# Gated experts in transposed form: a tile's input weights copied by ScalarE and held stationary

## The reference

```python
def _L2_ffn_ref(hidden_states, gate_w, gate_up_proj, down_proj):
    x = hidden_states.reshape(-1, H)
    probs = jax.nn.softmax(x @ gate_w.T, axis=-1)
    w, idx = jax.lax.top_k(probs, TOP_K)
    w = w / jnp.sum(w, axis=-1, keepdims=True)
    combine = jnp.zeros((T, E), x.dtype).at[jnp.arange(T)[:, None], idx].add(w)
    def step(acc, inputs):
        gup, dn, ce = inputs
        g, u = jnp.split(x @ gup.T, 2, axis=-1)
        acc = acc + ce[:, None] * (jax.nn.silu(g) * u @ dn.T)
        return (acc, None)
...
x = x + jnp.tanh(g_ffn[2]) * _L2_ffn_ref(_layernorm(x, axis=-1), L2_ffn_gate_w, L2_ffn_gate_up_proj, L2_ffn_down_proj)
```

## Time and profile before

| | |
|---|---|
| median of 3 runs | 841.63 us (841.47 to 844.58) |
| the profiled execution, whole | 842.73 us |
| its span, first to last instruction | 840.9 us |
| mean granted TensorE clock | 0.919 of full |
| layer-2 gated stage, first gather to last scatter's issue | 479.35 to 561.64 us |
| layer-3 gated stage, the same | 754.09 to 827.65 us |
| busy: TensorE, its weight loads, VectorE | 81%, 63%, 50% of the span |
| busy: ScalarE, GpSimd | 35%, 27% of the span |

### The profile page before, as it was taken

How to read it: one execution, slowest core, us unless ns; L and a number is a source line. 1 busy time by engine, 2 the same in 40 slices (tenths; PEclk the granted TensorE clock), 3 DMA queues, 4 the chain that set the end, 5 groups by cost and what they waited for, 6 DMA issues and landing times. The chain is left out here.

```text
span 840.9 us, 15319 instructions
## 1 busy us (share of the span) xinstructions
PE 677.8 (81%) x5100; PEld 532.3 (63%) x5101; DVE 419.4 (50%) x1095; ACT 291.2 (35%) x827; POOL 229.4 (27%) x275
## 2 busy tenths in 40 slices
PE   3988789677989999996898899961967999887772
PEld 2657677357879999985467756640544676674431
DVE  3585447684645344426695533325654454352233
ACT  1286123574024533530441033320631444312220
POOL 2033000132144444221001156523500111116652
PEclk9999999799899999998996999995996999889896
DMA  7980000000210001001930111110000000001123
GB/s 236 336 324 2 1 0 1 1 2 1 64 45 20 27 21 26 14 17 55 364 102 1 32 38 41 41 49 21 2 1 1 2 3 2 1 29 45 41 41 91
DMA packets 28998, 44.96 MB, mean 53 GB/s; under 512 B 5458, under 2 KB 18402, under 8 KB 28674
## 3 DMA queue, kind: packets, MB, share of 16 engines
q1 hardware_dynamic: 24514, 35.02, 12.4%
q0 software_dynamic: 4416, 9.05, 4.1%
HBM read 37.44 MB, written 6.62 MB: 52 GB/s over the span
## 5 line engine op out<-in xcount | busy, mean ns | idle before, releaser
L1120 PE MATMUL experts_ps<-experts_act,experts_own 128*128 128x128 f32 x736 | 86.0, 275 | 0.0
L1120 PEld LDWEIGHTS experts_ps<-experts_act,experts_own 128*128 128x128 f32 x736 | 84.0, 192 | 0.1
L1278 PE MATMUL gated_ps_in<-experts_w_in,gated_slots_t 128*128 x138 | 71.1, 624 | 14.0 <-DVE gated_slots_t L1365 5.9
L1167 ACT ACTIVATE experts_act<-experts_ps,experts_b 128x128 f32<-128x128 f32 x184 | 52.6, 369 | 73.0 <-PE experts_ps L1120 52.1
L1050 POOL DMA_INDIRECT gated_slots<-ffn_tokens,keep_ffn_token x46 | 44.5, 968 | 69.4 <-issue 44.8
L648 POOL TENSOR_TENSOR core_e<-core_e,core_inverse 128x1024 f32<-128x1024 f32 x16 | 30.4, 1902 | 105.8 <-DVE core_inverse L794 105.8
L1197 DVE COPY experts_own<-experts_w 128x2048 f32 x23 | 28.2, 1227 | 57.4 <-PE experts_ps L1120 57.4
L1365 DVE COPY gated_slots_t<-gated_ps_x 128x128 f32<-128x128 f32 x46 | 13.4, 291 | 85.4 <-PE gated_ps_x L1270 70.4
L1041 POOL DMA_INDIRECT ffn_results<-gated_results,keep_ffn_row x46 | 45.4, 986 | 36.8 <-DVE gated_results L1375 28.6
L1050 POOL DMA_INDIRECT experts_slots<-ffn_tokens,keep_ffn_token x23 | 36.1, 1570 | 65.7 <-PE experts_ps L1101 43.6
L1297 PEld LDWEIGHTS gated_ps_y<-experts_w_out,gated_gated_t 128*128 128x128 f32 x276 | 35.3, 195 | 24.7 <-issue 24.7
(11 more groups left out here) (398 smaller groups left out, 1432.7 us busy)
## 6 DMA issues: line engine op xcount, KB each, us to landing
experts_w<-in_L_ffn_W SPq DMA_DIRECT2D x1, 8192.0 KB, 40.8
experts_w_in<-in_gated_in SPq DMA_DIRECT2D x1, 4096.0 KB, 12.2
combine_mine<-ffn_results SPq DMA_DIRECT2D x12, 256.0 KB, 3.6
experts_w<-in_L_ffn_W SPq DMA_DIRECT2D x1, 2048.0 KB, 13.1
experts_w_out<-in_gated_out SPq DMA_DIRECT2D x1, 2048.0 KB, 16.7
ffn_tokens<-route_xn SPq DMA_DIRECT2D x3, 512.0 KB, 3.2
experts_w_in<-in_L_ffn_gate_w SPq DMA_DIRECT2D x1, 1024.0 KB, 19.5
experts_w_in<-in_L_ffn_up_w SPq DMA_DIRECT2D x1, 1024.0 KB, 23.0
```

What stands on the lines that cost most here:

```text
L1120: mm = pe.matmul(ps_2[u][:, c * P:(c + 1) * P], own2[:, u, k, c * P:(c + 1) * P], act1[:, u, k, :], start=(k == 0), stop=(k == chunks - 1))
L1167: act.activation(to[:, u, c, :], source[u][:, c * P:(c + 1) * P], ACT.Gelu, bias=bias[:, bass.ds(e * chunks + c, 1)]).then_inc(done, 1)
L1278: mm = pe.matmul(ps_in[:, banks * u + n], slots_t[:, u, :], w_in[:, bass.ds(e, 1), 512 * n:512 * n + 512].rearrange("d a h -> d (a h)"), s ...
```

## The change

Only `gated_experts` changes, with two helpers that go. The input matmuls change roles: for each 128 gate or up columns the weights are stationary and the turned slots stream, so the result comes out transposed already, gate and up columns on the partitions. `turn`, `gated_t`, `ps_t` and `keep_gated` go. The stationary weights come from `own`, a buffer of two tiles that ScalarE fills by copying the tile's 1024 (layer 3: 512) columns out of `w_in`, at first for tiles 0 and 1 and then, behind each silu(j), for tile j + 2, once the input matmuls of tile j are done. TensorE loads an expert index only in `down`, ScalarE one for each copy. The outputs have two PSUM banks. VectorE's order is now multiply(j), keep_result(j - 1), keep_slots(j + 2), and TensorE's up(j + 1), turn_slots(j + 2), down(j). All tiles are written out; there are no hardware loops.

```diff
@@ gated_experts @@
-        gated, gated_t = s.sb("gated", [P, 2, width]), s.sb("gated_t", [P, 2, chunks, P])
+        own, gated = s.sb("own", [P, 2, 2 * chunks, P]), s.sb("gated", [P, 2, chunks, P])
-        ps_in = s.psum("ps_in", [P, 2 * banks, 512])
-        ps_x, ps_t, ps_y = s.psum("ps_x", [P, 512]), s.psum("ps_t", [P, 512]), s.psum("ps_y", [P, 512])
+        ps_in = s.psum("ps_in", [P, 2, banks * 512])
+        ps_x, ps_y = s.psum("ps_x", [P, 512]), s.psum("ps_y", [P, 2, 512])
...
-                def up(j, u, first=False):
-                    e = expert_index(pe, routes, j)
+                def up(j):
+                    if j >= TILES:
+                        return
                     pe.wait_ge(sem["slots_kept"], j + 1)
-                    if not first:
+                    pe.wait_ge(sem["own_kept"], j + 1)
+                    if j >= 2:
                         pe.wait_ge(sem["gated_ready"], j - 1)
-                    for n in range(banks):
-                        mm = pe.matmul(ps_in[:, banks * u + n], slots_t[:, u, :],
-                                       w_in[:, bass.ds(e, 1), 512 * n:512 * n + 512].rearrange("d a h -> d (a h)"),
+                    for c in range(2 * chunks):
+                        mm = pe.matmul(ps_in[:, j % 2, c * P:(c + 1) * P], own[:, j % 2, c, :], slots_t[:, j % 2, :],
                                        start=True, stop=True)
                     mm.then_inc(sem["in_made"], 1)
 
-                def turn(j, u, first=False):
+                def down(j):
+                    e = expert_index(pe, routes, j)
                     pe.wait_ge(sem["gated_ready"], j + 1)
-                    if not first:
-                        pe.wait_ge(sem["gated_kept"], j)
+                    if j >= 2:
+                        pe.wait_ge(sem["result_kept"], j - 1)
                     for c in range(chunks):
-                        mm = pe.transpose(ps_t[:, c * P:(c + 1) * P], gated[:, u, c * P:(c + 1) * P], keep.identity[:])
-                    mm.then_inc(sem["gated_turned"], 1)
...
+                        mm = pe.matmul(ps_y[:, j % 2, 0:D], gated[:, j % 2, c, :],
                                        w_out[:, bass.ds(e, 1), c, :].rearrange("d a h -> d (a h)"),
                                        start=(c == 0), stop=(c == chunks - 1))
...
+                turn_slots(0)
+                up(0)
+                turn_slots(1)
+                turn_slots(2)
+                for j in range(TILES):
+                    up(j + 1)
+                    if j:
+                        turn_slots(j + 2)
+                    down(j)
...
+                def own_weights(j):
+                    if j >= TILES:
+                        return
+                    e = expert_index(act, routes, j)
+                    if j >= 2:
+                        act.wait_ge(sem["in_made"], j - 1)
+                    act.activation(own[:, j % 2].rearrange("d c h -> d (c h)"),
+                                   w_in[:, bass.ds(e, 1), :].rearrange("d a h -> d (a h)"), ACT.Copy)\
+                        .then_inc(sem["own_kept"], 1)
...
+                act.wait_ge(loaded, loads)
+                own_weights(0)
+                own_weights(1)
+                for j in range(TILES):
+                    silu(j)
+                    own_weights(j + 2)
...
+                keep_slots(0)
+                keep_slots(1)
+                multiply(0)
+                keep_slots(2)
+                for j in range(1, TILES):
+                    multiply(j)
+                    keep_result(j - 1)
+                    keep_slots(j + 2)
+                keep_result(TILES - 1)
```

More of the change, by code:

```diff
@@ L1012 @@
 AHEAD = 4
-def turn_ahead(turn_slots, i, v):
-    return [lambda n=3 + 2 * v + u: turn_slots(AHEAD * i + n, n % AHEAD, i + n // AHEAD) for u in range(2)]
-def pairs_of_tiles(engine, first, last, step):
-    pairs = (last - first + 1) // 2
-    with engine.Fori(0, pairs) as i:
-        for u in range(2):
-            step(first + 2 * i + u, (first + u) % 2)
-    for j in range(first + 2 * pairs, last + 1):
-        step(j, j % 2)
 def expert_index(engine, routes, j):
@@ L1291, in down @@
-                def down(j, u, first=False):
-                    e = expert_index(pe, routes, j)
-                    pe.wait_ge(sem["gated_kept"], j + 1)
-                    if not first:
-                        pe.wait_ge(sem["result_kept"], j)
-                    for c in range(chunks):
-                        mm = pe.matmul(ps_y[:, 0:D], gated_t[:, u, c, :],
+                        mm = pe.matmul(ps_y[:, j % 2, 0:D], gated[:, j % 2, c, :],
                                        w_out[:, bass.ds(e, 1), c, :].rearrange("d a h -> d (a h)"),
@@ L1300, in down @@
                     mm.then_inc(sem["result_made"], 1)
[L1302 removed]
+                idle_matmuls(pe, keep, ps_y[:, 0], 14)
                 pe.wait_ge(loaded, loads)
[L1304 to L1318 removed]
@@ L1390, in _ @@
-                steady(0)
-                with dve.Fori(1, (TILES - 3) // AHEAD) as i:
-                    steady(i)
-                j = TILES - 2
-                multiply(j + 1, 0)
-                for n in range(j - 1, TILES):
-                    keep_result(n, n % AHEAD, n // AHEAD)
+                    wait_scattered(dve, keep, routes, j % AHEAD, j // AHEAD)
+                    dve.tensor_copy(results[:, j % AHEAD, :], ps_y[:, j % 2, 0:D]).then_inc(sem["result_kept"], 1)
+                keep_slots(0)
```

96 lines of the change are left out of this document (21 added, 75 removed).

## The result

The changed kernel took 831.37 us (median of 4 runs, 829.18 to 834.67), the kernel before 841.80 beside it: a ratio of 0.9867 (95% interval 0.9837 to 0.9896), 10.4 us faster. The forecast was 819.7 us, 22 us faster, with a range of 815 to 829: the direction was right, the gain was too large, and the time lies outside the range.

A forecast was written before the change was run, and what follows sets the result against it. Layer 2 was taken as bound by TensorE, layer 3's middle by GpSimd. From 842.73 us, 11.3 (layer 2) and 10.6 (layer 3) came off, giving 820.8, or 819.7 on the median's scale; range 815 to 829.

The forecast's parts named there:

- Layer 2's sum: Layer 2 on TensorE: 25 passes, 2.79 us a tile, 0.37 less; with the tail, last scatter 11.3 us earlier.
- The pass of 0.1116 us: TensorE matmul pass with its own weights, weight load hidden, priced from the ungated experts stage at 0.1116 us.
- Hidden, by 0.22: Layer 2: the turn and down give 1.00 us, covering the 0.78 us slots wait with 0.22 to spare.
- the slots wait of 0.78 us: Before the next input matmuls: turn to copy start 0.34, copy 0.29, copy to matmul 0.15, together 0.78 us.
- rival B: Layer 2 stays at 3.16 us a tile, slots wait or ScalarE copy replacing the turn; 827.1 us, chance 0.14.
- Layer 3's stalls: Three standstills of every engine in layer 3, cause unknown, summing to 4.33 us, 3.4 above the usual 0.30.
- GpSimd's cycle: Layer 3 bound by GpSimd's 2.58 us a tile: 15 pairs and 7 scatters, 47.7 us first to last scatter.
- take them as staying: Layer 3's standstills kept at 3.4 us, so the stage gains 10.6 us; without them 13.9.
- ScalarE's copy: Copy of 1024 weight columns a tile in layer 2, taken as 1.04 us and hidden with about 1 us cover.
- rival D: ScalarE's copies hold up GpSimd's issues: 842.3 us with one issue held 0.87, 874.5 with both; chance 0.05.
- rival E: Weight loads not hidden, a pass costs twice: 5.6 us a tile in layer 2, about 895 us; chance 0.01.
- The clock (C): TensorE falls to 1.2 GHz in layer 3, giving 825.7 to 828.7 us; chance 0.12.

The follow-up runs named there:

- r5: The changed kernel once more, unedited, in a set with signals on time: 820.97 us, 0.9826 of the kernel before.
- r8: The kernel before once more, unedited, for its trace in a set with signals on time: 836.6 us.
- r6: The kernel before with its hardware loops in the gated stages written out, nothing else changed, signals on time: 828.62 us, 0.9931 of the kernel before.
- r2: The changed kernel with slots turned one tile earlier and three slots_t buffers, signals on time: 815.98 us, 0.976 of the kernel before.
- s4: The changed kernel with slots turned one tile earlier and three slots_t buffers, signals late: 833.73 us, 0.9887 of the kernel before.
- s3: The changed kernel without TensorE's expert index load (expert 0's output weights for every tile), signals late: 836.26 us, 0.9925 of the kernel before.

## Why the prediction was wrong

**Layer 2's sum held, its cover didn't.** The pass of 0.1116 us, 25 passes, 2.79 us a tile: r5 shows exactly that, and with the tail a stage 11.2 us shorter (83.26 to 72.10) against 11.3 forecast. The step that failed is "Hidden, by 0.22": the slots wait of 0.78 us was taken from a tile with the signal on time. Where a signal is held, the wait grows by 0.8 us on about every second tile, and the cover takes only 0.22 of it; that is 4.3 us in the stage. The kernel before showed no held signal in layer 2, at 3.16 us a tile, so that stage held no warning; its layer 3 did, in the stalls. What came is rival B, the slots wait in the place of the turn, at some 3.05 us a tile (tiles 3 to 19) instead of its 3.16.

**Layer 3's stalls were mis-sized, and its base was not understood.** GpSimd's cycle gives 47.7 us from first to last scatter; r5 has 47.49. The step that failed is "take them as staying", at 3.4 us: the changed kernel lost 8.9 in the late condition. The 3.4 counted only GpSimd's three long waits; r8 shows that late signals cost the kernel before 7.6 us there. The forecast thus let the change win back 4.2 us of a loss that in truth grew. Between first and last scatter the two stages took 61.73 and 56.39 us where the forecast has 57.3 and 51.1: 4.4 and 5.3 us, nearly all of the 9.5 us by which the profiled execution missed.

**The end of the loops was given no price.** I costed matmuls, copies and waits and overlooked that written-out code is an edit of its own. With signals on time it is 5.0 of layer 3's 5.9 us (r6, r5), since it takes TensorE from 2.60 to 2.17 us a tile; what it is worth where signals are late wasn't measured.

**What held.** ScalarE's copy takes 1.06 us (1.04 forecast) and the gather beside it 0.965: rival D is dead. By the rule of the Trainium skill weighed there ("SBUF — State Buffer", "Who interferes with whom"), ScalarE's copies leave GpSimd alone; the trace agrees. Weight loads of own weights hide behind the passes: rival E is dead. The clock (C) matters little: from first to last scatter of layer 3 it was granted 0.91, against 0.94 before. This window of the first trace, behind a standstill, was granted 0.68 (columns as in the earlier trace rows), a later one 0.95:

```profile
781.00:784.00 3.00, 2.57 (x14) 2.57 (x15) 1.54 (x5) 1.78 (x4) 2.07 (x3) 0.68 0.08 22
785.00:790.00 5.00, 2.91 (x22) 2.59 (x20) 1.06 (x4) 1.10 (x3) 2.94 (x3) 0.95 0.19 52
```

Where signals are on time the kernel took 820.97 us, close to the 819.7 forecast; but there the kernel before took 835.88 and the gain was 14.9 us, not 22. So the agreement is luck in part, two errors that cancel: the stalls that the forecast kept and the loss that its base held.

**What stays open:** what in the chip or its surroundings makes the condition, and by what way indirect transfers delay TensorE's signals to three other engines. That it isn't VectorE's order, TensorE's index load, the slots' cover, or the phase of signal and scatter alone is shown. Three things weren't tried: the written-out kernel before in the late condition, a kernel that issues its indirect transfers 1.6 us apart or more there, and a time taken without the profiler's records. No correct kernel tried here beats the changed one in both conditions: r2 is 816.0 us with signals on time and level with it where they are late.

## What to carry to other kernels

A standstill of all engines in the profile isn't a constant to carry over: ask which signals are late at that moment, and count a new tight wait as paid if its cover is shorter than the longest delay seen anywhere in the trace. Longer cover isn't a cure either: a whole tile of it brought nothing here (s4). Run the unchanged kernel beside every experiment, since three different edits seemed to cure what the next set of runs brought back. And price each edit in the diff, the end of a loop too: here, with signals on time, it was 7.3 of 14.9 us by the medians and 5.0 of 17.0 by the stages of single traces.

## What the runs showed of the hardware

- Where signals are on time, silu starts 0.20 us behind the end of the input matmuls (r5; 0.35 in one tile). In the late condition it starts up to 3.0 us behind them in the changed kernel and 3.7 in s3, while GpSimd issues indirect transfers in turn, gathers and scatters or gathers alone. Two signals between other engines were not late: VectorE's product started 0.03 us behind silu's end in every trace wherever it waited for it (505.96 to 505.99), and in the changed order TensorE started 0.05 to 0.06 us behind a slots' copy that it waited for (509.36 to 509.42).
- In that condition a pair of gather and scatter settles at 2.96 us in layer 3 (2.57 otherwise) and at 3.05 to 3.15 in layer 2; at the 3.16 us a tile of the kernel before in layer 2 nothing is held.
- The same program leaves 6687 semaphore updates in its trace where signals are on time and 5623 or 5664 where they are late.
- Written-out loops save 0.43 us a tile in layer 3 of the kernel before (2.60 against 2.17), and nothing in layer 2 (stages of 83.26 and 83.22 us), where TensorE has no gap.
- A ScalarE copy from SBUF to SBUF takes 1.06 us for 1024 columns of fp32 and 0.63 for 512. A plain transfer issued by GpSimd holds it for 0.6 us, an indirect one for 0.97. A `memset` of 0.33 us between two of its issues lengthens its cycle by 0.2 us.
